# A graph attention layer before a mixture of experts: one norm per node batch, the residual product moved beside the edges, and an edge stage of fp32 one-hots with its weights in PSUM

## The reference

```python
x = x + gnn(layernorm(x));  x = x + moe(layernorm(x))
# gnn, of the normed x:
xn = layer_norm(x, ln1_g, ln1_b)                # so x is normed twice, the second time with gain and bias
h = (xn @ W).reshape(N, 8, 32)
a_src, a_dst = einsum(h, att_src), einsum(h, att_dst)          # one number per node and head
e = leaky_relu(a_src[src] + a_dst[dst], 0.2)                   # edges, and one loop per node
alpha = softmax of e over the edges of each dst
out = segment_sum(h[src] * alpha, dst) + xn @ W_res + bias
out = layer_norm(out, ln2_g, ln2_b);  gnn = out + gelu(out @ w1 + b1) @ w2 + b2
# moe: 8 experts 256 -> 1024 -> 256, the top 2 of each node by a softmax router
```

## Time and profile before

| | |
|---|---|
| median of 3 runs | 2603.32 us (2600.9 to 2607.2) |
| the profiled execution | 2595.19 us, span 2593.9 us |
| PE / PEld busy | 1978.6 us (76%) / 1742.4 us (67%) |
| DVE busy | 1715.1 us (66%) |
| ACT busy | 1440.7 us (56%) |
| POOL busy | 1272.6 us (49%) |
| mean granted TensorE clock | 0.842 of full |
| DMA | 356.45 MB, mean 137 GB/s |

### The profile page before, as it was taken

One profiled execution on the slowest core, in us unless ns is written; L12 is line 12 of the kernel. 1 busy time (PEld: TensorE's weight loads), 2 busy tenths in 40 slices (PEclk: granted clock), 3 DMA queues, 4 the chain that ended last, 5 costly groups with the idle time before them and its releaser, 6 DMA issues.

```text
span 2593.9 us, 50933 instructions
## 1 busy us (share of the span) xinstructions
PE 1978.6 (76%) x16716; PEld 1742.4 (67%) x16716; DVE 1715.1 (66%) x5377; ACT 1440.7 (56%) x3220; POOL 1272.6 (49%) x1168
## 2 busy tenths in 40 slices
PE   4773667666666666666656999998499999998995
PEld 3552555555555555555544888888499999998995
DVE  6654889888888888888877777664344444443442
ACT  1234656555556555655553677664356656665562
POOL 1217777777777777777770133333222222232321
PEclk9895777777777777777777999998699999999998
DMA  3446655555555555655553122211654453437534
GB/s 97 133 126 152 182 164 158 162 161 158 160 157 157 162 160 160 174 160 160 162 171 99 58 86 97 83 57 58 219 170 113 109 172 75 140 95 249 153 64 121
DMA packets 191790, 356.45 MB, mean 137 GB/s; under 512 B 42007, under 2 KB 126834, under 8 KB 182566
## 3 DMA queue, kind: packets, MB, share of 16 engines
q0 software_dynamic: 63840, 151.61, 24.2%
q1 hardware_dynamic: 127110, 200.50, 22.6%
q10 hardware_dynamic: 576, 1.09, 0.1%
HBM read 431.75 MB, written 95.50 MB: 203 GB/s over the span
## 4 chain that ended last, share of the span: by engine, by line
POOL 37%; PE 29%; issue 17%; DMA 5%; DVE 5%; ACT 4%; SPq 1%; DVEq 0%; POOLq 0%; ACTq 0%
POOL edge_mem L724 34%; PE bank L1034 8%; PE bank L1035 8%; PE bank L1036 8%; DMA expert_mem<-expert_rows 4%; POOL expert_rows L1208 1%; ACT layer_hid L1130 1%; DVE edge_mem L383 1%; PE bank L1746 1%; ACT layer_mem L1129 1%; DVE stats L374 1%; ACT layer_mem L1138 1%; POOL rstd L387 1%; PE bank L1293 1%; PE bank L483 1%
## 5 line engine op out<-in xcount | busy, mean ns | idle before, releaser
L724 POOL DMA_INDIRECT edge_mem<-node_table,src_col x880 | 905.4, 1029 | 277.2 <-issue 267.9
L869 PE MATMUL bank<-edge_mem 128*128 128x264 f32 x1760 | 533.6, 464 | 18.5 <-DVE win_mem L961 13.7
L1034 PE MATMUL bank<-expert_rounded 128*128 128x256 f32 x1792 | 517.3, 289 | 0.0
L1035 PE MATMUL bank<-expert_rounded 128*128 128x256 f32 x1792 | 512.2, 286 | 0.0
L1036 PE MATMUL bank<-expert_rounded 128*128 128x256 f32 x1792 | 512.0, 286 | 0.0
L869 PEld LDWEIGHTS bank<-edge_mem 128*128 128x128 f32 x1760 | 394.3, 233 | 136.3 <-issue 53.1
L1732 POOL DMA_INDIRECT sums<-expert_mem,slot_tok x112 | 189.6, 1693 | 546.4 <-DVE expert_mem L1670 462.3
L1030 DVE TENSOR_TENSOR expert_rounded<-expert_mem,expert_rounded 128x512 fp32r<-128x512 f32 x280 | 194.0, 693 | 282.2 <-ACT expert_rounded L1719 216.8
L1719 ACT ACTIVATE expert_mem<-bank,par 128x256 f32<-128x256 f32 x448 | 228.6, 510 | 265.4 <-PE bank L1036 265.4
L1034 PEld LDWEIGHTS bank<-expert_rounded 128*128 128x128 f32 x1792 | 349.7, 195 | 0.1
L1035 PEld LDWEIGHTS bank<-expert_rounded 128*128 128x128 f32 x1792 | 349.5, 195 | 0.0
(11 more groups left out here) (233 smaller groups left out, 3889.5 us busy)
## 6 DMA issues: line engine op xcount, KB each, us to landing
expert_rounded<-split_w SPq DMA_DIRECT2D x224, 1024.0 KB
split_w<-piece_hi SPq DMA_DIRECT2D x72, 256.0 KB
split_w<-piece_lo SPq DMA_DIRECT2D x72, 256.0 KB
piece_full<-in_L_ffn_W SPq DMA_DIRECT2D x64, 256.0 KB
expert_mem<-expert_rows SPq DMA_DIRECT2D x56, 265.0 KB, 3.6
edge_mem<-node_table,src_col POOLq DMA_INDIRECT x880
node_table<-win_mem SPq DMA_DIRECT2D x12, 544.0 KB, 3.0
out<-sums SPq DMA_DIRECT2D x1, 6250.0 KB, 21.7
```

Of the source, the lines that this page charges most:

```text
L724: pool.indirect_dma_start(gath[g % NGB][:, t, :], None, node_table, bass.IndirectOffsetOnAxis(ap=src_col[:, k, t % 2:t % 2 + 1], axis=0)). ...
L869: ins = pe.matmul(bank[5 + at % 3][:, 0:AGG], onehot[g % 2][:, 2 * k + j, :], gath[g % NGB][:, 2 * k + j, 0:AGG], start=(j == 0), stop=(j ...
L1034: pe.matmul(out_ap, s_hi, m_lo, start=start, stop=False)
L1035: pe.matmul(out_ap, s_lo, m_hi, start=False, stop=False)
```

## The change

Node stage: x is loaded before the weights. The two norms become one: variance v is turned into v * (1 + EPS) + EPS * EPS ahead of the inverse root, and the rows are normalized once. The residual product, its bias and its store leave the stage; instead SP stores xnT in `turned`. `COLS` is (7, 8, 10), these transposes use banks 5 and 6, and PE makes h behind them instead of ahead of the next batch's turn. SP no longer waits for `step_win` in round 2, but in round 6.

Edge stage: the one-hots are fp32. The turned one is no longer made by PE: SP spreads the group's 2048 dst numbers (bf16) over all partitions, and ACT makes Abs and Relu over them. The splits in three bf16 parts are gone: 16 fp32 matmuls each take the place of twice 48 bf16 ones. The running maxima of the eight steps of a group are one scan over 64 numbers with flags `same`; copies from and to the window are ACT's. `wgt` and the factor (`shrink`) lie in PSUM. `messages` has four pieces of four tiles, each behind one `scale_and_add`. One tile of the residual product is made per group. POOL waits for the table alone, and at group 2 for `turned`. Sources are taken one round earlier (group n+1 in round g).

```diff
@@ node stage
+        def node_stats(b):
+            ...
+            dve.tensor_scalar(mv[:, 0:n, 1], mv[:, 0:n, 1], 1.0 + EPS, EPS * EPS, ALU.mult, ALU.add).then_inc(stats_ready, 1)
+        def node_norm(b):
+            dve.wait_ge(root_ready, b + 1)
+            ... ins = dve.tensor_scalar(xt, xt, mv[:, j, 0:1], root[:, j:j + 1], ALU.subtract, ALU.mult)
         def nodes_sp():
+            load_x(0)
             ...
+            load_x(1)
+            for i in range(1, NB + 2):
+                if i + 1 < NB:
+                    load_x(i + 1)
+                if i <= NB:
+                    store_turned(i - 1)
                 if i >= 2:
+                    store_table(i - 2)
                 prep_sp(i)
         def edges_pool():
             pool.wait_ge(table_written, n_table)
             pool.wait_ge(cols_copied, 2 * NK * 3)
-            pool.wait_ge(residual_written[0], 16 * ((NB + 1) // 2))
-            pool.wait_ge(residual_written[1], 16 * (NB // 2))
@@ edge stage
+        wgt = bank[3][:, 0:GT * HEADS].rearrange("p (t h) -> p t h", h=HEADS)
+        shrink = bank[4][:, 0:HEADS * GS].rearrange("p (h k) -> p h k", k=GS)
         def edges_sp():
+                sp.dma_start(dst_row, step_dst[r, :]... .to_broadcast([P, GS * EB])).then_inc(rows_spread[g % 2], 16)
+                sp.dma_start(same[g % 2][:, :], step_same[g, :, :]... .to_broadcast([P, HEADS * GS])).then_inc(...)
+                next_residual(g - 2)
+        def residual_product(w):
+            pe.wait_ge(scored, w + 1)
+            for k in range(KC):
+                pe.matmul(b_res, xn_in[:, k * P:(k + 1) * P], Wres[:, k, :], start=(k == 0), stop=False)
+            pe.matmul(b_res, ones[0:1, :], bias_row[0:1, :], start=False, stop=True).then_inc(res_made, 1)
         def edges_act():    # one round
+                if n < NG:
+                    one_hot(n)                  # 16 Abs of 128x128, one Relu of 128x2048, fp32
+                    ... act.copy(cand...) twice, the second behind cand_turned
+                if 0 <= g < NG:
+                    act.activation(wgt, score[:, :, :], ACT.Exp).then_inc(weights_ready, 1)
+                    keep_maxima(g)              # 8 copies into the window, each waited for
+                if n < NG:
+                    take_nodes(n)               # 8 copies out of the window
+                if n + 1 < NG:
+                    take_sources(n + 1)
+                if n < NG:
+                    for i in pieces_of(n): high_piece(i)
+                    one_hot_turned(n)           # Abs and Relu of 128x2048
+                if 0 <= g < NT:
+                    keep_residual(g)
+                if 0 <= g < NG:
+                    act.wait_ge(added, GS * g)
+                    act.activation(shrink, scale[g % 2][:, :, :], ACT.Exp).then_inc(scale_ready, 1)
         def edges_pe():     # one round
+                asrc transposes(n); sum_step(g - 1, 0..3)
+                    for t in range(GT):
+                        ins = pe.matmul(b_edge[:, t * 16:(t + 1) * 16], onehot_t[g % 2][:, t * P:(t + 1) * P],
+                                        nodeval[g % 2][:, :, :, t // 2], start=True, stop=True)
+                cand transposes(n); sum_step(g - 1, 4..7); residual_product(g)
+                            ins = pe.matmul(b_ms[:, k * 9:(k + 1) * 9], onehot[n % NOH][:, 2 * k + j, :], cand[:, j, k, :], ...)
         def edges_dve():    # one round
+                    node_chain(g)               # 11 small operations, one behind the other
+                    tensor_tensor_scan(seg_max...); scale_and_add(g - 1, 0); mask; scale_and_add(g - 1, 1); low_piece
+                    scale_and_add(g - 1, 2..3); scores (4 operations, behind edge_vals)
+                for m in range(4):
+                    scale_and_add(g - 1, GS // 2 + m)
+                    messages(g, m)
```

More of the change, by code:

```diff
@@ L129, in build @@
         gath = [part(i * GT * ROW, GT, ROW) for i in range(NGB)]
[L130 to L135, removed]
+        onehot = [part(OH0 + i * GT * P, GT, P) for i in range(NOH)]
+        onehot_t = [part(OT0 + i * GT * P, GT * P) for i in range(2)]
@@ L454, in nodes_pool @@
+        def node_norm(b):
+            _, mv, root = node_sum[b % 2]
+            dve.wait_ge(root_ready, b + 1)
+            for j in range(tiles_of(b)):
+                xt = xs[b % 3][:, j, :]
+                ins = dve.tensor_scalar(xt, xt, mv[:, j, 0:1], root[:, j:j + 1], ALU.subtract, ALU.mult)
+            ins.then_inc(normed, 1)
         def nodes_pool():
@@ new lines, in edges_sp, with load_xn, store_residual, next_residual @@
+            next_residual(NG - 1)
+        def load_xn(w):
+            if w >= 1:
+                sp.wait_ge(res_made, w)
+            sp.dma_start(xn_in[:, :], turned[w, :, :]).then_inc(xn_loaded, 16)
+        def store_residual(w):
+            sp.wait_ge(res_kept, w + 1)
+            sp.dma_start(residual[w * P:(w + 1) * P, :], res_out[:, :]).then_inc(residual_written, 16)
+        def next_residual(w):
+            if 0 <= w < NT:
+                store_residual(w)
+                if w + 1 < NT:
+                    load_xn(w + 1)
@@ L928, in node_chain @@
-                dve.tensor_tensor(parts[:, 2, :, :], rest[:, :, :], parts[:, 1, :, :], ALU.subtract).then_inc(parts_ready, 1)
+                dve.wait_ge(nodes_taken, g + 1)
+                v(dve.tensor_tensor(topped[:, :], newm[:, :], nv_max, ALU.max))
+                dve.wait_ge(rows_spread[g % 2], 32 * (g // 2 + 1))
+                if g >= 1:
+                    dve.wait_ge(maxima_kept, GS * g)
+                dve.tensor_tensor_scan(run[:, 0, 1:], same[g % 2][:, :], topped[:, :], -BIG, ALU.add, ALU.max).then_inc(running_ready, 1)
@@ new lines, in node_chain @@
+                dve.wait_ge(running_ready, g + 1)
+                v(dve.tensor_tensor(before[:, :], run[:, 0, 0:HEADS * GS], same[g % 2][:, :], ALU.add))
+                v(dve.tensor_tensor(run[:, 1, 1:], before[:, :], nv_max, ALU.max))
+                v(dve.tensor_tensor(summit[:, :, :], run[:, :, 1:], nv_dst.unsqueeze(1).to_broadcast([P, 2, HEADS * GS]), ALU.add))
+                dve.scalar_tensor_tensor(nv_max, summit[:, 0, :], SLOPE, summit[:, 0, :], ALU.mult, ALU.max).then_inc(nodeval_ready, 1)
```

696 lines of the change are left out of this document (337 added, 359 removed).

## The result

The changed kernel takes 2909.9 us (2901.5 to 2926.3) beside 2603.3 us: 1.118 times as long, 95% interval 1.113 to 1.124, or +307 us. Forecast were 2492 us and a chance of 0.08 for slower.

The account below looks back on a forecast made before the run. POOL's instruction stream of gathers was taken to bound the edge stage. Node stage -70 and edge stage -41 us made -111 on 2603.3, so 2492 us, with 0.80 between 2462 and 2560.

Parts of the forecast that it names:

- the line on DMA: Edge stage: 512 KB more dst a group and 256 KB residual traffic, share 0.57 to some 0.7, hidden.
- the term of 4 us: Edge stage: PE's clock mostly full, with 4 us added over the stage for rounds where it isn't.
- A: The forecast case: T 20.2 to 20.7, first gather at 108 to 132, 2470 to 2521 us, chance 0.50.
- Rival C: Edge stage: PE at half the clock through nearly half its work, T = 23, slower at 2634 us, chance 0.07.
- T: Edge stage: length in us of one round, that is one group of 16 gathers; forecast 20.35.
- 45 + 54 T + 26.5: Edge stage length if engines set the round: 45 us start, 54 rounds, 26.5 for the last two.
- Gathers: Edge stage: with L935 and L957 reading PSUM, POOL's gathers average under 0.97 us, -53 us.
- The inference of the Trainium skill: Rival on gathers: descriptor generation is not held up by `tensor_tensor`, taking 53 us out of the gain; 2542 us.
- Engines' paces: Edge stage: DVE 18.5, PE 17.2 and ACT 18.9 us a round, all under POOL's 20.35.
- Node stage: Stage before the gathers: first gather at 120 instead of 190.8 us, -70 us.
- One lap of two batches: Node stage, norm to norm two rounds on: 5.8 us product, 4.8 x landing, 3.5 statistics and norm, 14.1 us.
- rival D: Node stage held by DMAs and SP's order, first gather at 145, 2516 us; or gathers stay 1.33, 2542; chance 0.13.

Follow-up runs that it names:

- e1: The changed kernel with SP issuing seg_new and seg_last ahead of its wait for the turned one-hots and ahead of dst: 2521.6 us, 0.9645 of the kernel before.
- e6: The changed kernel with eight unread products of 128x256 fp32 put ahead of PE's fourth running sum: 2765.7 us, 1.0624 of the kernel before.
- e3: The kernel before with the softmax weights alone in PSUM, both halves of the turned one-hots going through one bank: 2553.4 us, 0.9782 of the kernel before.
- e11: The kernel of e7 with softmax weights and scalings in SBUF again, run in the slower condition: gathers 1063 ns in the mean; its time is not given.
- e17: The kernel of e7 unchanged, run again in the condition where the kernel before takes 3469 to 3494 us: 3414 us.
- e7: The kernel of e1 with a fourth buffer for x in the node stage, each load issued one batch sooner: 2500.8 us, 0.959 of the kernel before.
- e5: The changed kernel with seg_new and seg_last issued just ahead of dst, still behind SP's wait for the turned one-hots: 2747.8 us.

## Why the prediction was wrong

*The step that failed* is the line on DMA: "the spread dst is 512 KB more a group ... hidden". The bytes are hidden (share 0.67 in e1, 0.7 forecast); their place in a queue was not. The rows for the scan were given no term at all. The round was followed for DVE, PE and ACT, and never for SP, although SP got a wait for the end of ACT's round (`oht_ready`, a single `dst_row`) ahead of two small loads that DVE needs first. DVE's wait for these rows is 3.5 us a group, 190 us over 54 rounds, and a group took 27.2 us for 20.35. No engine's sum of work contains that ring. Moving two lines gives 388 us back, more than the whole loss.

*The clock.* "PE would stand still twice for some 2 us. So I expect it mostly full, and add 4 us": the clock was 0.69 in the stage, the edge values took 6.65 us for 3.3, and e6, which keeps the clock up through them, gives 144 us back. So the term of 4 us was far too small. The rows behind it had gaps, but none of the new small fp32 products. The Trainium skill (TensorE: Matmul & The Clock Gate, "HAM oscillation — how this bites in real kernels") tells of a kernel whose TensorE waits for data in each turn of its loop and begins each turn at the low clock; the trace of the changed kernel agrees for the edge values, at 0.50 behind their gap. The falls at 937 there, and in e1 from 884 and 894, come with PE busy throughout and are of another kind. What makes those was not tested. In e1 the granted clock is 0.81 in the stage with PE 94% busy; so "above 0.9 in A" was wrong too, at no cost, as POOL sets the pace.

*Rival C* named the effect (edge stage by PE at half the clock, slower than before) and gave 2634 for T = 23. With T = 27.2 its own formula, 45 + 54 T + 26.5, gives 1540 us; measured 1566. Its chance of 0.07 was too small: the prediction said itself that it would be wrong if DVE, exposed to waits in two thirds of its round, stood still more than 2 us a group, and had priced no wait but those between the three engines. Its cause, PE by itself at half the clock, is not what the runs show: the ring was the cause, and the clock a part of its length.

*Gathers: right.* Mean 957 ns for "under 0.97", and e3 gives 58 us for "-53", with L957 still on two SBUF inputs. The inference of the Trainium skill (SBUF — State Buffer, "Who interferes with whom") that spares `tensor_tensor` beside descriptor generation was a rival; for these gathers the measurements decide against it (1029 to 966 ns in e3, 1063 against 948 in e11 and e17).

*Engines' paces: right once the rows come in time.* 20.3 us a group in e1 for 20.35, the fp32 products at the full clock 3.64 us for 3.3; end of the edge stage 52 us after the last gather for 49.

*Node stage: -41 for -70.* One lap of two batches was forecast at 14.1 us. In the changed kernel x's transfers on the chain of waits begin at 59.83, 78.46, 99.79 and 126.52:

```profile
59.83 5.54 DMA edge_mem<-in_x
...
78.46 5.99 DMA edge_mem<-in_x
...
92.81 6.06 PE bank L511 x16
```

18.6 to 26.7 us a lap: the transfer 5.0 to 6.0 for 4.8, the product 4.6 to 6.1 for 3.7, and in each lap a preparation step. Here, too, the length of the ring was SP's order (x behind the table); e7 opens it and lands at 123.8. The half of rival D on the node stage (145, by SP's order) was the right one (149.4 in the changed kernel, 147.4 in e1); with the edge stage as forecast it had 2516, and e1 took 2521.6.

*The rest* grew by 9.4 us in the changed kernel, 14.6 in e1 and 11.6 in e7, at a clock of 0.92 to 0.93 for 0.94. Why wasn't tested.

## What to carry to other kernels

Follow the round for the engine that issues the DMAs as for those that compute: write down what each load waits for and what stands behind that wait, and ask for the smallest load behind the largest one. SP issues in the order of its program, so one wait for one single buffer was a wait for everything behind it. A gap on PE is to be priced at two clocks: what followed it on this ring took 6.65 us for 3.64. And when every engine's sum lies under the round, look for the wait that occurs once in each round, however small it is among the totals.

## What was not expected of the hardware

Two 64 KB loads issued just behind a 512 KB one were usable 4.8 us after issue, ahead of it within 2.9 and 3.2 in two rounds of e5. Filling idle PE time with useless products made the kernel 5% faster. The clock fell to 0.50 with PE busy throughout (e1). PE 98% busy was not the bound. And the kernel before took 2607 us and, later on the same chip, 3479. Of e7's kernel, 2501 and 3414 us there, both traces exist: DVE, ACT and POOL have the same busy time within 5 us, but DVE stands idle 7.2 us in the mean before it reads the maxima, in the round shown for 9 us behind the end of PE's records. In that condition the changed kernel and the kernel before are equal within 0.3%, so the order of two versions can depend on it.
